# A decoder layer on one core: a program with a loop over batches against one written out for four batches, with smaller attention tiles, other bank assignments and norms folded into later steps

## What is computed

```python
x = x + rms_norm(lightning_attn(rotary(h @ Wq), rotary(h @ Wk), h @ Wv)) @ Wo          # h = layernorm(x)
#   16 heads of 16; causal, each score times r**(i - j) with a decay r of its head; written with a state:
#   inter = (q * q_decay) @ kv;  intra = ((q @ k.T) * dmask) @ v;  kv = r**C * kv + (k * k_decay).T @ v   (C = 128)
kv  = ctx @ W_k.T + b_k                                    # p = layernorm(x)
sim = einsum('bid,bjd->bij', einsum('bij,bjd->bid', p, kv), kv) / 16
x = x + softmax((sim - mean) * rsqrt(var + 1e-6) * gamma + beta)
logits = h @ Wr;  top 2 of 8 experts, gate = softmax of the two     # h = layernorm(x)
x = x + sum_e gate[e] * (h @ We[e] + be[e])
```

## Time and profile before

| | us |
|---|---|
| median of 3 runs | 174.38 (174.18 to 174.51) |
| the profiled execution | 174.52 |
| its span, first to last instruction | 172.3 |
| PE busy | 152.0 |
| DVE busy | 123.4 |
| ACT busy | 61.5 |
| POOL busy | 32.2 |

### The profile page before, as it was taken

The page is one execution under the profiler, slowest core; times in us unless marked ns, Lnnn a source line. Parts: engine busy times, 40 slices in busy tenths (PEclk is TensorE's granted clock), DMA queues, the critical chain, the costliest instruction groups (busy, mean ns, idle before and its releaser), DMA issues.

```text
span 172.3 us, 3040 instructions
## 1 busy us (share of the span) xinstructions
PE 152.0 (88%) x981; PEld 104.0 (60%) x981; DVE 123.4 (72%) x401; ACT 61.5 (36%) x171; POOL 32.2 (19%) x53
## 2 busy tenths in 40 slices
PE   0999999799779899999779899998698899998991
PEld 0555458257436778678248787675376667636880
DVE  0523593887899889757899597668996557877762
ACT  3265846055850320537712202469203120410100
POOL 4103200314320032045200130423100204010030
PEclk9999999999999999999999999999999999999998
DMA  5999400002000000000040000000100000001001
GB/s 150 313 351 348 104 0 4 0 4 76 0 4 0 0 4 0 2 0 0 0 122 22 0 0 0 0 0 0 61 0 0 2 0 0 0 0 61 4 0 61
DMA packets 7930, 7.29 MB, mean 42 GB/s; under 512 B 2264, under 2 KB 7664, under 8 KB 7792
## 3 DMA queue, kind: packets, MB, share of 16 engines
q1 hardware_dynamic: 7424, 6.79, 12.6%
...
...
## 4 chain that ended last, share of the span: by engine, by line
PE 49%; DVE 27%; issue 7%; ACT 6%; DVEq 5%; DMA 2%; POOL 2%
PE bank L793 13%; PE ebank L793 12%; DVE probs L624 7%; PE ebank L801 4%; PE bank L841 4%; ACT qx L426 3%; DVE stats L520 2%; PE bank L923 2%; DMA cst<-in_consts 2%; PE bank L881 2%; PE bank L808 2%; DVE w_e_lo L585 2%; DVEq L521 2%; DVE norm L531 2%; POOL rs L326 2%
## 5 line engine op out<-in xcount | busy, mean ns | idle before, releaser
L624 DVE TENSOR_TENSOR probs<-bank,dec 128x512 f32<-128x512 f32 x32 | 19.8, 680 | 1.6 <-PE bank L881 1.6
L326 POOL TENSOR_TENSOR rs<-ve,nhalf 128x2 f32<-128x2 f32 x16 | 12.1, 756 | 37.1 <-DVE ve L525 37.0
L881 PE MATMUL bank<-qx,kT 64*128 64x512 f32 x64 | 18.0, 624 | 0.8 <-ACT kv L481 0.8
L801 PE MATMUL ebank<-cst 128*128 128x512 f32 (+1 forms) x22 | 11.5, 645 | 4.7 <-DMA cst<-in_consts 4.7
L558 DVE SCALAR_TENSOR_TENSOR acc<-ebank,gate,acc 128x256 f32<-128x256 f32 x26 | 11.3, 477 | 3.2 <-PE ebank L793 3.0
L793 PE MATMUL ebank<-w_e_hi,h3T_hi 128*128 128x512 f32 x40 | 13.4, 416 | 0.2 <-DVE w_e_lo L585 0.2
L426 ACT ACTIVATE qx<-bank,cst 128x256 f32<-128x256 f32 x32 | 12.6, 487 | 0.0
L558 DVE SCALAR_TENSOR_TENSOR acc<-bank,gate,acc 128x256 f32<-128x256 f32 x22 | 9.3, 478 | 4.5 <-PE bank L793 3.0
L793 PE MATMUL ebank<-w_e_hi,h3T_lo 128*128 128x512 f32 x40 | 12.5, 394 | 0.0
L793 PE MATMUL ebank<-w_e_lo,h3T_hi 128*128 128x512 f32 x40 | 12.4, 392 | 0.0
L326 POOL TENSOR_TENSOR rms_rs<-rms_ve,nhalf 128x2 f32<-128x2 f32 x4 | 3.1, 785 | 46.1 <-DVE rms_ve L768 46.1
...
## 6 DMA issues: line engine op xcount, KB each, us to landing
...
```

What stands on the lines that cost most here:

```text
L326: nc.gpsimd.tensor_tensor(dst[:], src[:], nhalf[:], ALU.pow).then_inc(done, 1)
L624: nc.vector.tensor_tensor(probs[:, t, 4 * n:4 * n + 4, :], bank[2 + n][:].rearrange("p (h n) -> p h n", h=4), dec[:, 4 * n:4 * n + 4, :], ...
L801: pe.matmul(dst[:, 0:cols], ident, cst[:, 0:cols], start=True, stop=True)
L881: pe.matmul(bank[2 + n][:], kT[rows, t, g, :], qx[rows, t, g, :, :], start=True, stop=True).then_inc(s_sc_ps, 1)
```

## The change

The program is written out for the four batches, without a loop. Per batch there are three chains: a front (norm of x, projections, rotation, transposes, scores' operands and states), a middle (scores, attention, residual, similarities, softmax) and the experts. The front has the PSUM banks `front[0]` and `front[1]`, the middle has `chain` (four banks, written and read also as one), the experts have two `ebank`; for batch 0 and 1 parts of the front borrow others. Front, middle and experts in one turn of the Python loop `for b in range(1, B)` belong to batches b + 1, b and b - 1.

Attention works in chunks of 64 tokens (`CH`), with three states a batch. A score product has 32 rows (one pair of heads), 64 output rows and 128 columns, 16 in a tile, so that ACT lays q out twice and DVE multiplies two pieces of 128x512 per tile by the decay. `attend` has 64 products of 64 rows and 64 columns, and 24 of 32 rows with the states; `states` has 32 products of 32 columns; their keys are decayed on POOL in four versions.

The norms: x is centred (on DVE for batch 0, on ACT after), and its reciprocal deviation becomes the scale of the ACT copies of q, k and v. The second norm's mean is removed on ACT, the keys of the context are centred instead of the similarities, and the variance comes from ACT's squares with an accumulated sum; the third norm's scale goes into the exponent of the gate and into the gates that the experts' products are multiplied with. Inputs have a buffer for each batch and are loaded ahead. 15 of the 18 `keep_clock` matmuls are gone, and the three left have 256 columns. Both halves of the experts' weights are split in pieces of 1024 columns on ACT.

```diff
-        bank = [stack.enter_context(nc.psum_tensor(f"bank{n}", [P, 512], F32)) for n in range(6)]
+        front = [stack.enter_context(nc.psum_tensor(f"front{n}", [P, 512], F32)) for n in range(2)]
+        chain = stack.enter_context(nc.psum_tensor("chain", [P, 4, 512], F32))
         ebank = [stack.enter_context(nc.psum_tensor(f"ebank{n}", [P, 512], F32)) for n in range(2)]
...
+        att_ps = chain[:, 0:HALVES, 0:D]
...
-        def passes(eng, body):
-            body(0, True, False, False)
-            body(1, True, True, False)
-            with eng.Fori(2, B) as i:
-                body(i, True, True, True)
-            body(B, False, True, True)
-            body(B + 1, False, False, True)
...
+            for b in range(B):
+                if b == 0:
+                    for t in range(TILES):
+                        rotary_cross(1, t)
+                if b + 2 < B:
+                    x_rstd(b + 2)
+                rms_rstd(b)
+                if b == 0:
+                    keys_for_states(1)
+                x1_variance(b)
+                if 0 < b < LAST:
+                    for t in range(TILES):
+                        rotary_cross(b + 1, t)
+                sim_rstd(b)
+                if 0 < b < LAST:
+                    keys_for_states(b + 1)
+                if b:
+                    add_biases(b - 1)
+                x2_rstd(b)
+            add_biases(LAST)
...
+            def head_queries(b, t):
+                act.wait_ge(s_qkT_ps, TILES * b + t + 1)
+                if b:
+                    act.wait_ge(s_sc_ps, 2 * TILES * b)
+                src = qk_bank(b, t)
+                act.copy(kT[:, t], src[:, D:].rearrange("p (g n) -> p g n", g=GROUPS))
+                for k in range(2):
+                    o = act.activation(qx[:, t, :, k, :], src[:, 0:D].rearrange("p (g n) -> p g n", g=GROUPS),
+                                       ACT.Copy, scale=cst[:, C_PICK + k:C_PICK + k + 1])
+                o.then_inc(s_qkT, 1)
...
+            def center_x1(b, t):
+                act.wait_ge(s_nmu3, b + 1)
+                if b:
+                    act.wait_ge(s_x2, TILES * b)
+                    act.wait_ge(s_ve2, b)
+                act.activation(x1c[:, t], x1[:, t], ACT.Identity, bias=nmu3[:, t:t + 1]).then_inc(s_x1c, 1)
+                act.activation(squares1[:, t], x1[:, t], ACT.Square, bias=nmu3[:, t:t + 1],
+                               accum_out=ssq1[:, t:t + 1]).then_inc(s_sq1, 1)
...
+            def square_similarities(b, t):
+                act.wait_ge(s_sim, b + 1)
+                act.activation(squares[:, t], sim_ps(t), ACT.Square, accum_out=ssq[:, t:t + 1]).then_inc(s_sq, 1)
...
+            def decay_scores(b, t):
+                if b == 0:
+                    dve.wait_ge(s_dec, 16)
+                else:
+                    dve.wait_ge(s_at_ps, b)
+                for n in range(2):
+                    dve.wait_ge(s_sc_ps, 2 * (TILES * b + t) + n + 1)
+                    rows = slice(2 * n, 2 * n + 2)
+                    nc.vector.tensor_tensor(probs[:, t, rows], chain[:, rows, 0:D],
+                                            dec[:, rows], ALU.mult).then_inc(s_sc, 1)
...
+            def softmax_input(b):
+                dve.wait_ge(s_gam, 32)
+                dve.wait_ge(s_nbet, 1)
+                dve.wait_ge(s_sr, b + 1)
+                for t in range(TILES):
+                    nc.vector.scalar_tensor_tensor(out=zg[:, t], in0=sim_ps(t), scalar=sim_rs[:, t:t + 1],
+                                                   in1=gam[:], op0=ALU.mult, op1=ALU.mult).then_inc(s_zg, 1)
+                for t in range(TILES):
+                    dve.wait_ge(s_zg, TILES * b + t + 1)
+                    nc.vector.tensor_tensor_reduce(out=zb[:, t], in0=zg[:, t], in1=nbet[:], scale=1.0,
+                                                   scalar=3.0e38, op0=ALU.add, op1=ALU.min,
+                                                   accum_out=nmax[:, t:t + 1]).then_inc(s_nm, 1)
...
+            for b in range(1, B):
+                x2_low(b - 1, 0)
+                x2_low(b - 1, 1)
+                if b == 1:
                     low_experts(1)
...
+                if b + 2 < B:
+                    x_stats(b + 2)
+                route(b - 1)
+                add_experts(b - 1, 0)
+                rms_variance(b)
+                residual1(b)
+                add_experts(b - 1, 1)
+                if b < LAST:
+                    x_low(b + 1, 0)
+                    x_low(b + 1, 1)
+                sim_variance(b)
+                if b < LAST:
+                    rotate(b + 1, 0)
+                softmax_input(b)
+                if b < LAST:
+                    rotate(b + 1, 1)
+                    decay_queries(b + 1, 0)
+                add_experts(b - 1, 2)
+                residual2(b, 0)
+                residual2(b, 1)
+                if b < LAST:
+                    decay_queries(b + 1, 1)
+                    decay_scores(b + 1, 0)
+                    decay_scores(b + 1, 1)
+                add_experts(b - 1, 3)
+                if b < LAST:
+                    mask_states(b + 1)
...
+            def states(b):
+                pe.wait_ge(s_kd, TILES * (b + 1))
+                pe.wait_ge(s_v, TILES * (b + 1))
+                pe.wait_ge(s_qkT, TILES * b + 1)
+                pe.wait_ge(s_qd, TILES * b + 1)
+                for t, v, n in ((0, 0, 0), (0, 1, 1), (0, 2, 2), (1, STATES, 2)):
                     for g in range(GROUPS):
...
+                        for q in range(PAIRS):
+                            pair = vpad[b % 2][:, t].rearrange("p (k a) n -> p k (a n)", a=2)[:, g * PAIRS + q]
+                            pair = pair.rearrange("p (u n) -> p u n", n=DH)[:, 0:4:3, :]
+                            at = (n * GROUPS + g) * 2 * DH
+                            first_mm = n < 2 or (v == 2 and g == 0)
+                            mm = pe.matmul(qk_bank(b, 0)[32 * q:32 * q + 32, at:at + 2 * DH],
+                                           kd[:, v, g * P + 32 * q:g * P + 32 * q + 32], pair,
+                                           start=first_mm, stop=(n < 2 or (v != 2 and g == GROUPS - 1)))
+                mm.then_inc(s_state_ps, 1)
...
+                for n in range(2):
+                    if t:
+                        pe.wait_ge(s_sc, 4 * b + n + 1)
                     for g in range(GROUPS):
...
+                        for c in range(HALVES):
+                            half = slice(c * CH, (c + 1) * CH)
+                            for r in (2 * n, 2 * n + 1):
+                                rows = slice(32 * r, 32 * r + 32)
+                                mm = pe.matmul(chain[half, r, g * P:(g + 1) * P], kT[rows, t, g, half],
+                                               qx[rows, t, g, :, half], start=True, stop=True)
...
+                for t in range(TILES):
                     for g in range(GROUPS):
+                        cols = slice((t * GROUPS + g) * CH, (t * GROUPS + g + 1) * CH)
                         for par in range(2):
...
+                            at = slice((2 * g + par) * CH, (2 * g + par + 1) * CH)
+                            for c in range(HALVES):
+                                half = slice(c * CH, (c + 1) * CH)
+                                for q in range(PAIRS):
+                                    pe.matmul(chain[32 * q:32 * q + 32, c, cols],
+                                              vpad[b % 2][half, t, g * 8 + q * 2 + par, :], probs[half, t, q, at],
+                                              start=(t == 0 and g == 0 and par == 0), stop=False)
+                for n in range(STATES):
+                    t, c = divmod(n + 1, HALVES)
                     for g in range(GROUPS):
...
+                        cols = slice((t * GROUPS + g) * CH, (t * GROUPS + g + 1) * CH)
+                        for q in range(PAIRS):
+                            rows = slice(32 * q, 32 * q + 32)
+                            mm = pe.matmul(chain[rows, c, cols], state[b % 2][rows, n * GROUPS + g, :],
+                                           qd[b % 2][rows, t, g, c * CH:(c + 1) * CH], start=False,
+                                           stop=(n > 0 and g == GROUPS - 1))
+                mm.then_inc(s_at_ps, 1)
...
+            keep_clock(chain[:, 2], 256)
+            keep_clock(chain[:, 3], 256)
+            keep_clock(chain[:, 2], 256)
...
+            for b in range(1, B):
+                transpose_x2(b - 1, 0)
+                transpose_x2(b - 1, 1)
+                attend(b)
+                logits(b - 1)
+                expert(b - 1, 0, 0)
+                expert(b - 1, 0, 1)
+                square_sums(b)
+                project(b, 0)
+                project(b, 1)
+                transpose_gates(b - 1)
+                expert(b - 1, 1, 0)
+                bias_product(b - 1)
+                transpose_x1(b, 0)
+                transpose_x1(b, 1)
+                expert(b - 1, 1, 1)
```

(27 more changed lines are left out.)

1496 lines of the change are left out of this document (796 added, 700 removed).

## The result

The changed kernel takes 184.5 us (median of 4 runs, 182.89 to 186.11) against 174.4 of the kernel before, a ratio of 1.054 with a 95% interval of 1.046 to 1.062. I had forecast 167.2, with a range of 155 to 177. The profiled execution took 186.11 us, 184.3 of it span, so it is 1.6 us above the median. Medians in this document are over all runs of a kernel, while the ratios leave out its slow runs (over 1.5% above its fastest), so that the two can differ by a microsecond or more, and where they do the ratio counts.

The account below looks back on a forecast made before the run. Neither PE nor DVE alone was the bound, but chains handed from engine to engine. Stages 49.4 + 37.2 + 35.4 + 27.1 + 16.0 gave 165.1 us of span; plus 2.2 less 0.1, 167.2 us, range 155 to 177.

Parts of the forecast that it names:

- Part 1: Small products on PE: attention 2.4 us a batch (1.5 to 4.7), scores 1.9 us less, states 0.9 us.
- Rival B: Attention and states on PE: a pass costs 27 ns whatever its size, attention 4.7 us, time 174.9 us; chance 0.15.
- the 2 to 3 that I had named as the sign: Expected profile sign: the 176 PE passes of an attention take 2 to 3 us; 4.5 or more would favour B.
- Part 4, the third quarter: Loop turn, 35.4 us in all: third-quarter expert unit waits for DVE's third add and runs 28.1 to 29.5 us.
- Part 3, the start: Start up to the first expert unit: x2's transposes at 49.4 us, first unit at 52.3 instead of 62.15.
- my walk: Step-by-step timing of the engines' instruction lists through start, turns and end, giving 167.2 us; chance 0.43 that it holds.
- Rival D: PE's clock falls to 1.2 GHz in idle stretches of start and last turn, 9 to 10 us, time 177; chance 0.12.
- 49.4, 37.2, 35.4 and 27.1: Forecast stage lengths in us: start to x2's transposes, first turn, second turn, last turn up to batch 3's experts.
- my 16.0: Forecast length in us of the tail: batch 3's expert units, gates and biases, three adds and the store.

Follow-up runs that it names:

- the pair above: Changed kernel with reordered turns and start plus fillers, 168.0 us; the same with tiny matmuls placing one end of PE's 256-record fetch blocks in each attention, 163.8 us.
- the fillers: Changed kernel with 22 more executed filler matmuls in PE's own waits, no wait of the work changed: 174.9 us, ratio 1.003 to the kernel before.
- the biases stand early: Changed kernel with POOL adding the experts' biases ahead of x1's variance: 177.6 us, ratio 1.018; with the fillers too, 175.4 us, ratio 0.981.
- The fastest kernel: Changed kernel with turns and start reordered, fillers, fetch block ends placed and some of DVE's low parts and statistics moved behind batch 0's routing: 161.9 us, ratio 0.927.

## Why the prediction was wrong, step by step

- **Part 1 held for the products and missed their supply.** I took 2.4 us for an attention. The one without a stop, of batch 2, takes 2.6 (98.40 to 101.01) at a granted clock of 1.00; in batch 0's the first 128 products take 1.48, 11.6 ns each eight side by side, and the 48 with the states 18 ns each in batch 2's, and scores and states fit too. Rival B is out. So is the 25 ns between starts that the Trainium skill gives (TensorE: Matmul & The Clock Gate, "Wait — 56ns, not 53.3ns?"), for products on different parts of the array. But with their stops the other three attentions take 4.1 to 4.4 us, outside the 2 to 3 that I had named as the sign. What Part 1 did not ask is what 1767 matmuls instead of 981 cost besides their columns. They cost the gaps of the fetch, 4.2 us in the pair above (3.1 by the ratios): a price with no row of before, which I had put at nothing.
- **Part 4, the third quarter.** "rotation of tile 1 (0.4 + 0.45) 26.5; four adds": I walked POOL's list to the similarities' power and no further. The biases two entries later were the step that DVE waited for: 3.8 us at a held clock, 6.9 with what the clock adds.
- **Part 3, the start**: 55.98 for 49.4. x1 came at 38.3 instead of 34.5. Attention of batch 0 started at 28.8 instead of 25.9 with the clock at 0.5 from 20.5 to 27.3 us (with the fillers, at 1.00, it started at 26.2), and a fetch gap of 1.6 stood in it; the low parts that waited for a cast were in my walk. Then PE idled 3.3 us before the context product: the context's copy stood on ACT behind two steps that nobody needed yet, 1.3 us long; I had that order and did not price it.
- **Rival D was the mechanism, in the wrong place and too small.** I gave the clock 0.12, confined to the start and the last turn, 9 to 10 us. That the total matches (9.6 us by the fillers) is luck: the last turn ran at a granted clock of 1.00, and the clock fell in the full turns, for which I had priced no fall. It did not need the gaps that I had missed: in the first turn the fall comes right behind the 2.0 us before the last transposes of q and k, a gap that my own walk has (the quarter's second unit ends at about 24 in it, the rotation at 26.5), and in both turns it still comes there when the biases stand early. I had held stretches longer than the 1.58 us of the earlier trace rows against the clock in the start and the last turn only, and not in the full turns.
- **The sum closes, in part by luck.** 184.5 less 9.6 (fillers), 3.8 (biases, clock held) and 4.2 (fetch) is 166.9, against 167.2; by the ratios alone it is 167.9. The three were measured on different bases and each holds some clock. The kernel nearest to my walk, with fillers and the biases early but the power behind the rotation, took 171.4 us of span against my 165.1:

```profile
0.00:52.41 52.41, 43.04 (x570) 26.86 (x570) 22.90 (x71) 28.56 (x77) 14.57 (x32) 0.97 0.36 106
52.41:91.28 38.87, 34.06 (x454) 25.27 (x450) 25.27 (x85) 16.48 (x54) 9.16 (x15) 1.00 0.01 2
91.28:127.62 36.34, 33.68 (x450) 25.11 (x450) 20.24 (x71) 16.46 (x54) 8.00 (x14) 1.00 0.03 9
127.62:155.85 28.23, 25.68 (x293) 18.93 (x293) 14.77 (x59) 10.20 (x38) 4.54 (x8) 1.00 0.06 20
```

With a tail of 15.6 that is 3.0, 1.7, 0.9 and 1.1 us over my 49.4, 37.2, 35.4 and 27.1, and 0.4 under my 16.0; three fetch gaps of 1.5 to 1.8 us (in the start, the first turn and the last) are in it. So turns and tail were sized within 2 us once clock and biases are mended, and the start was too short by 3. The fastest kernel's stages are no test of the walk, since it has the power early, the start reordered and low parts moved, which the walk has not.

The steps that failed are three terms that the walk put at nothing: the clock in the full turns (with all that fillers mend elsewhere, 9 to 10 us), the biases behind the last decayed keys (3.8) and the fetch of 1767 matmuls (3 to 4). Behind them is one habit: the walk followed each chain to the step I was looking for, and priced PE's idle time at its own length. In this kernel a PE gap of 2 us costs more than 2: by fillers alone 9.6 us came back without any wait being shorter.
